# Banded window attention: softmax weights turned by a diagonal matrix of inverse row sums, V stationary, heads produced feature-major

## The reference

```python
h = shift_token(x); q, k, v = split(h @ wqkv)
q, k = l2norm(q) * qs, l2norm(k) * ksc
q, k = rotary_xpos(q, k)
sim  = einsum('bhwid,bhwjd->bhwij', 8 * q, k)   # masked to i-64 <= j <= i
attn = softmax(sim)
x    = x + reshape(attn @ v) @ wo
```

## Time and profile before

| | |
|---|---|
| median of 3 runs | 4411.17 us (4400.55 to 4414.39) |
| profiled execution | 4408.55 us |
| its span, first to last instruction | 4406.7 us |
| PE, DVE, ACT, POOL busy in the span | 78%, 74%, 54%, 57% |
| granted TensorE clock, mean | 0.897 of full speed |
| attention layer 0 of the changed function | about 1330 to 1615 us |
| attention layer 1 of the changed function | about 1670 to 1957 us |

### The profile page before, as it was taken

One profiled execution on the slowest core, in us unless ns is written; L12 is line 12 of the kernel. 1 busy time (PEld: TensorE's weight loads), 2 busy tenths in 40 slices (PEclk: granted clock), 3 DMA queues, 4 the chain that ended last, 5 costly groups with the idle time before them and its releaser, 6 DMA issues. The chain is left out here.

```text
span 4406.7 us, 82280 instructions
## 1 busy us (share of the span) xinstructions
PE 3422.4 (78%) x26525; PEld 2224.7 (50%) x26525; DVE 3282.7 (74%) x5820; ACT 2366.2 (54%) x5461; POOL 2504.6 (57%) x2258
## 2 busy tenths in 40 slices
PE   5888888888866876875879799765877776777775
PEld 3666666666654654654744577421433342333343
DVE  4777777777746865765641688678999977999995
ACT  3555555555533533442332566565777756767771
POOL 2555555555534524423420233348999965999991
PEclk8999999999977977877989899877999997999996
DMA  1000000000000000000000000017777745777760
GB/s 55 9 9 9 9 9 9 9 9 9 9 20 0 0 6 15 0 6 5 0 27 0 20 1 1 15 57 240 233 233 233 233 139 171 233 229 234 230 219 33
DMA packets 196676, 328.22 MB, mean 74 GB/s; under 512 B 96048, under 2 KB 126016, under 8 KB 194368
## 3 DMA queue, kind: packets, MB, share of 16 engines
q1 hardware_dynamic: 196288, 323.29, 23.7%
HBM read 304.30 MB, written 18.87 MB: 73 GB/s over the span
## 5 line engine op out<-in xcount | busy, mean ns | idle before, releaser
L3562 ACT ACTIVATE banks<-banks,alog 128x255 f32<-128x255 f32 x2048 | 788.6, 448 | 338.1 <-DVE h L3651 221.2
L3629 POOL TENSOR_TENSOR dBx<-residual,b_by_state 128x1024 f32<-128x1024 f32 x256 | 597.2, 2354 | 23.4 <-POOLq L3622 16.6
L3651 DVE TENSOR_TENSOR_SCAN h<-banks,dBx 128x1024 f32<-128x1024 f32 x256 | 579.8, 2281 | 35.9 <-PE banks L3491 19.7
L3629 POOL TENSOR_TENSOR norm_featmajor<-norm,b_by_state 128x1024 f32<-128x1024 f32 x256 | 597.9, 2357 | 0.5 <-DMA norm<-mamba_dtx_rows 0.5
L3651 DVE TENSOR_TENSOR_SCAN h<-banks,norm_featmajor 128x1024 f32<-128x1024 f32 x256 | 581.0, 2282 | 6.2 <-POOL norm_featmajor L3629 0.5
L3476 PE MATMUL banks<-dt_rows,selectors 128*128 128x510 bf16 x1024 | 418.0, 409 | 156.8 <-ACT banks L3562 96.3
L3491 PE MATMUL banks<-h,c_spread 128*32 128x128 f32 x8192 | 345.0, 289 | 25.0 <-DVE h L3651 18.6
L3491 PEld LDWEIGHTS banks<-h,c_spread 128*32 128x32 f32 x8192 | 203.7, 113 | 201.8 <-issue 154.4
L3474 PE MATMUL banks<-dt_rows,selectors 128*128 128x255 bf16 x512 | 151.7, 296 | 138.8 <-ACT banks L3562 134.5
L973 POOL TENSOR_TENSOR weighted<-probs,f 128x1024 f32<-128x1024 f32 x64 | 120.8, 1904 | 215.3 <-DVE f L1024 214.2
L3476 PEld LDWEIGHTS banks<-dt_rows,selectors 128*128 128x128 bf16 x1024 | 110.0, 107 | 248.2 <-ACT banks L3562 169.4
(11 more groups left out here) (455 smaller groups left out, 8994.3 us busy)
## 6 DMA issues: line engine op xcount, KB each, us to landing
residual<-mamba_dtx_rows SPq DMA_DIRECT2D x512, 256.0 KB, 3.5
norm<-mamba_dtx_rows SPq DMA_DIRECT2D x512, 256.0 KB, 3.4
mamba_dt_rows<-dt_parts SPq DMA_DIRECT2D x8, 768.0 KB, 3.4
dt_rows<-mamba_dt_rows SPq DMA_DIRECT2D x32, 192.0 KB, 4.8
delta_blocks<-A_turned SPq DMA_DIRECT2D x256, 8.0 KB, 1.5
inv_turned<-delta_blocks SPq DMA_DIRECT2D x256, 8.0 KB, 1.8
mamba_dtx_rows<-dtx SPq DMA_DIRECT2D x16, 256.0 KB, 3.7
c_spread<-in_l3a_zero SPq DMA_DIRECT2D x2, 1160.0 KB, 6.4
```

Source lines behind the costliest of these rows:

```text
L3562: e = fn(per_step(decay[l % 2])[:, 2 * x + j, 1:], k.bank[x][:, j * T + 1:(j + 1) * T], ACT.Exp, scale=mem["A"][:, at:at + 1])
L3629: nc.gpsimd.tensor_tensor(per_step(dBx[l % 4]), per_step(kept[l % 4]), across(mem["B"][:, tokens(tb)], 4), ALU.mult).then_inc(q["dbx"], 1)
L3651: v.tensor_tensor_scan(flat(h[:, u % 2, 4 * i:4 * i + 4, :]), decay[l % 2], dBx[l % 4], 0.0, ALU.mult, ALU.add).then_inc(q["scanned"], 1)
```

## The change

The turned softmax weights leave TensorE already divided by their row sums: the block of E is multiplied, as the stationary operand, by a diagonal matrix `dg` with the inverse row sums, in place of the identity. DVE inverts the sums, GpSimd multiplies the identity by them (8 diagonals of 128 x 128 for a unit, one buffer for all units). `heads_of` takes v as the stationary operand and streams ET, so the heads come out feature-major in bank 7 and go to OT by one copy; `turn_out`, `out` and the buffer O go. ACT takes over `load_x` and the third copy of ET. The orders on the engines change. The diff, cut:

```diff
 # PE
 def turn_probs(x0, b, u):
-    pe.wait_ge(q["exped"], b * NU + u + 1)
+    pe.wait_ge(q["dg_ready"], b * NU + u + 1)
...
-        i = nc.tensor.transpose(k.bank[TB + n // 4][...], E[:, u, n // 3, ...], k.ident[:])
+        i = nc.tensor.matmul(k.bank[TB + n // 4][...], E[:, u, n // 3, ...], dg[:, n // 3, (n % 3 + 1) // 2, :],
+                             start=True, stop=True)
 def heads_of(b, u):
-    pe.wait_ge(q["pt_act"], (b * NU + u) * 2 + 2)
-    pe.wait_ge(q["pt_dve"], b * NU + u + 1)
+    pe.wait_ge(q["pt_ready"], (b * NU + u) * 3 + 3)
...
-        nc.tensor.matmul(hout[:, 0, h, :], ET[:, u, 3 * h, :], v[:, 0, vh], start=True, stop=True)
-        nc.tensor.matmul(hout[:, 1, h, :], ET[:, u, 3 * h + 1, :], v[:, 0, vh], start=True, stop=False)
-        i = nc.tensor.matmul(hout[:, 1, h, :], ET[:, u, 3 * h + 2, :], v[:, 1, vh], start=False, stop=True)
+        o = k.bank[7][h % 2 * DK:(h % 2 + 1) * DK, h // 2 * T:(h // 2 + 1) * T]
+        nc.tensor.matmul(o, v[:, 0, vh], ET[:, u, 3 * h:3 * h + 2, :].rearrange("p a t -> p (a t)"),
+                         start=True, stop=False)
+        i = nc.tensor.matmul(o[:, P:T], v[:, 1, vh], ET[:, u, 3 * h + 2, :], start=False, stop=True)
-def turn_out(b, u): ...
 def step(x0, x1, x2):
-    turn_out(x2, 0)  heads_of(x2, 1)  project(x0, 0)  turn_qk(x1)  project(x0, 1)  score(x1, 0)
-    turn_out(x2, 1)  score(x1, 1)  last_projection(x2)  turn_probs(x1, 0)  heads_of(x1, 0)  turn_probs(x1, 1)
+    heads_of(x2, 1)  project(x0, 0)  turn_qk(x1)  project(x0, 1)  score(x1, 0)
+    last_projection(x2)  score(x1, 1)  turn_probs(x1, 0)  heads_of(x1, 0)  turn_probs(x1, 1)
 # ACT
+def load_x(b):
+    after(act, "proj", b * TPB)
+    for lo, at in ((0, PAD), (64, PAD - 1)):
+        nc.scalar.activation(xb[lo:lo + 64, :], ..., ACT.Copy).then_inc(q["xb_ready"], 1)
 def copy_probs(b, u):
-    for n in (0, 1):
+    for n in range(3):
 def copy_out(b, u):
-    act.wait_ge(q["o_turned"], b * NU + u + 1)
+    act.wait_ge(q["heads"], b * NU + u + 1)
 def step(x0, x1, x2):
+    load_x(x0)
     move_v(x1)
+    copy_out(x2, 1)
     read_out(x0, 0)  copy_turned(x1, 0)  copy_turned(x1, 2)  read_out(x0, 1)
-    copy_out(x2, 1)
     exponentials(x1, 0)  copy_probs(x1, 0)  exponentials(x1, 1)
+    copy_out(x1, 0)
     copy_probs(x1, 1)
-    copy_out(x1, 0)
 # POOL: front(b) is cut into squares (L1766), lengths (L1769) and turned_part (L1774)
+def weights_of(b, u):
+    pool.wait_ge(q["inverted"], b * NU + u + 1)
+    after(pool, "p_turned", (b * NU + u) * 3)
+    g.tensor_tensor(dg[:].rearrange("p h t q -> p (h t) q"), across(k.ident[:], HG * TPB),
+                    over(rs[:, u].rearrange("p h t -> p (h t)"), P), ALU.mult).then_inc(q["dg_ready"], 1)
+def step(x0, x1):
+    squares(x0)  weights_of(x1, 0)  lengths(x0)  weights_of(x1, 1)  turned_part(x0)
-front(0)
+step(0, None)
 with pool.Fori(1, B) as b:
-    front(b)
+    step(b, b - 1)
+step(None, B - 1)
 # DVE: load_x, copy_probs and out go
+def weights_of(b, u):
+    dve.wait_ge(q["exped"], b * NU + u + 1)
+    vv.reciprocal(rs[:, u], rs[:, u]).then_inc(q["inverted"], 1)
 def step(x0, x1, x2):
-    load_x(x0)  normalised(x1)  out(x2, 0)  copy_probs(x2, 1)  rotated(x1)  out(x2, 1)  copy_turned(x1)
-    norms(x0, 0)  banded(x1, 0)  maxima(x1, 0)  norms(x0, 1)  banded(x1, 1)  add_y(x2)  maxima(x1, 1)  copy_probs(x1, 0)
+    normalised(x1)  weights_of(x2, 1)  rotated(x1)  copy_turned(x1)
+    norms(x0, 0)  banded(x1, 0)  maxima(x1, 0)  norms(x0, 1)  add_y(x2)  banded(x1, 1)  maxima(x1, 1)  weights_of(x1, 0)
```

More of the change, by code:

```diff
@@ L1546, in window_attention_layer @@
                  "v_moved", "read_out", "y_added",
-                 "rotated", "turned", "t_act", "t_dve", "scores", "maxed", "exped", "p_turned", "pt_act", "pt_dve", "heads",
-                 "heads_out", "o_turned", "ot_ready", "final", "s_read")
+                 "rotated", "turned", "t_act", "t_dve", "scores", "maxed", "exped", "inverted", "dg_ready", "p_turned", "pt_ready", "heads",
+                 "ot_ready", "final", "s_read")
         q = {n: p.sem(n) for n in names}
-        hout = k.bank[7].rearrange("p (t h d) -> p t h d", t=TPB, h=HG)
         def batches(eng, step):
@@ L1588, in project @@
                     if t == 0:
-                        pe.wait_ge(q["xb_ready"], b + 1)
-                        after(pe, "pt_act", (b - 1) * NU * 2)
-                        after(pe, "pt_dve", (b - 1) * NU)
+                        pe.wait_ge(q["xb_ready"], b * 2 + 2)
+                        after(pe, "pt_ready", (b - 1) * NU * 3)
                     else:
@@ L1626, in turn_probs @@
                     else:
[L1627 to L1628 removed]
+                        after(pe, "pt_ready", (b * NU + u) * 3)
                     for n in range(HG * 3):
[L1630 to L1631 removed]
+                        i = nc.tensor.matmul(k.bank[TB + n // 4][:, n % 4 * P:(n % 4 + 1) * P],
+                                             E[:, u, n // 3, n % 3 * P:(n % 3 + 1) * P], dg[:, n // 3, (n % 3 + 1) // 2, :],
+                                             start=True, stop=True)
                         if n % 4 == 3:
@@ L1677, in step @@
                     if x2 is not None:
-                        turn_out(x2, 1)
+                        last_projection(x2)
                     if x1 is not None:
                         score(x1, 1)
-                    if x2 is not None:
-                        last_projection(x2)
                     if x1 is not None:
@@ L1691, in _ @@
             def _(act):
+                act.wait_ge(q["loaded"], 80)
+                def load_x(b):
+                    after(act, "proj", b * TPB)
+                    for lo, at in ((0, PAD), (64, PAD - 1)):
+                        nc.scalar.activation(xb[lo:lo + 64, :], k.HT[lo:lo + 64, bass.ds(b, 1), at:at + T].rearrange("p a t -> p (a t)"),
+                                             ACT.Copy).then_inc(q["xb_ready"], 1)
                 def move_v(b):
@@ L1730, in step @@
                 def step(x0, x1, x2):
+                    if x0 is not None:
+                        load_x(x0)
                     if x1 is not None:
                         move_v(x1)
+                    if x2 is not None:
+                        copy_out(x2, 1)
                     if x0 is not None:
@@ L1761, in _, with squares @@
                 pool.drain()
-                def front(b):
+                def squares(b):
                     for t in range(TPB):
@@ L1774, in front @@
                             g.tensor_tensor(qk[:, t, a], qn[:, t, a], across(tab[:, t, a, 0, :], H), ALU.mult).then_inc(q["turned_part"], 1)
-                front(0)
+                def weights_of(b, u):
[4 more added lines that the diff above has]
+                def step(x0, x1):
+                    if x0 is not None:
+                        squares(x0)
+                    if x1 is not None:
+                        weights_of(x1, 0)
+                    if x0 is not None:
+                        lengths(x0)
+                    if x1 is not None:
+                        weights_of(x1, 1)
+                    if x0 is not None:
+                        turned_part(x0)
+                step(0, None)
                 with pool.Fori(1, B) as b:
-                    front(b)
+                    step(b, b - 1)
+                step(None, B - 1)
             @block.vector
@@ L1865, in step @@
                     if x2 is not None:
-                        out(x2, 0)
-                        copy_probs(x2, 1)
+                        weights_of(x2, 1)
                     if x1 is not None:
                         rotated(x1)
-                    if x2 is not None:
-                        out(x2, 1)
-                    if x1 is not None:
                         copy_turned(x1)
```

28 lines of the change are left out of this document (6 added, 22 removed).

## The result

The changed kernel takes 4508.34 us (median of 4 runs, 4504.49 to 4509.12) against 4407.05 for the kernel before (4 runs beside it): 1.0227 times as long, 95% interval 1.0204 to 1.0249. The prediction was 4576, range 4505 to 4640, slower with 0.95; the median lies 3 above the lower end of that range, and the difference is 101 where 165 was forecast. The profiled execution took 4507.62, span 4505.8, 99.1 more than the span before (4406.7).

A forecast was written before the change was run, and what follows sets the result against it. No engine was full; a ring of waits through POOL's power set the step. Steps of 42.0 us instead of 30.98 gave 77 a layer, plus 7 for each tail, less 3: 165 more, 4576 us, range 4505 to 4640.

The forecast's parts named there:

- diagonal 0: POOL's building of unit 0's diagonal, now ahead of the power while DVE stands idle: 1.9 us a step.
- the ring: Waits in each loop step that make all four engines work one after another: 42.0 us a step instead of 30.98.
- tail of 7 a layer: Work behind a layer's last power, with two diagonals and dearer turnings, less two output detours: +7 us.
- The start: Start of layer 0, where the input copy no longer waits for POOL's memset: -2.7 us.
- power, normalising, reciprocal 1: POOL's power 5.4, DVE's normalising with its drain 3.8 and unit 1's reciprocal 0.2: 9.4 us a step.
- diagonal 1: POOL's building of unit 1's diagonal beside DVE's rotation: 2.7 us, bounds 1.9 to 3.0.
- turning 1, up to the last copy: PE's 12 turnings of unit 1's softmax weights, multiplications instead of transposes: 3.1 us at full clock, transposes 1.5.
- heads: PE's heads of unit 1, 1536 columns alternating between halves of the array: 1.9 us, formerly 2.7.
- scores to reciprocal 0: From PE's first scores through DVE's bands, maxima and sums of squares to unit 0's reciprocal: 10.0 us a step.
- more hand-overs: Some nine hand-overs between engines, most inside other terms; 0.7 us more a step.
- The clock, 4.5: PE at half clock for about ten microseconds behind its waits, partly off the critical chain: 4.5 us a step.
- Clock holds: Rival: multiplying keeps PE at 2.4 GHz on the critical chain; 37.5 us a step, 4512 total; chance 0.14.

The follow-up runs named there:

- the run with the exponentials first: Changed kernel with POOL's power before diagonal 0 and ACT's exponentials of unit 1 ahead of its copies of unit 0; 4439.21 us.
- the run with the idle multiplications: Changed kernel with multiplications nobody reads ahead of PE's waits for diagonals (18 for unit 0, 10 for unit 1); 4490.23 us, ratio 1.0195 to the kernel before.

## Why the prediction was right, and what was mis-sized

The mechanism was the one forecast, and the rows that were to show it are there: the power behind diagonal 0 of 1.89, which waits for the reciprocal; DVE idle 7.47 before normalising; PE waiting 7.33 and 4.09 ahead of the turnings. Two that were named with them are not: the power's starts are 37.5 apart and not 42, and neither turning takes 3.1 (5.13 and 4.54). The runs confirm the ring from several sides: longer diagonals lengthen the step at their full price, with none to build or wait for it is 28.8, and an earlier hand-over shortens it, except that of the power alone, behind which ACT closed the ring. That the power's place on POOL is all of it (38.1 to 39.0 with the power first), that the turning's price is (28.8 with the multiplications kept) and that TensorE's clock is (36.5 with turning 1 at full clock), each of these fell with a run. The forecast's tail of 7 a layer was right: from the last power to the MEMSET of L1343 it is 59.76 and 59.74 instead of 53.19 and 52.70, so 6.6 and 7.0 more. The start came out at -0.8 for -2.7, which the spread of that start from run to run hides.

The step was put at 42.0 and is 37.55, and 14 x 4.45 = 62 is nearly all of the 68 by which 4576 was too high. By the terms:

| term | predicted | measured |
|---|---|---|
| diagonal 0 | 1.9 | 1.85 |
| power, normalising, reciprocal 1 | 9.4 | 9.5, of it 2.5 normalising, 1.2 a wait for ACT |
| diagonal 1 | 2.7 | 2.0 |
| turning 1, up to the last copy | 3.1 | 4.6 |
| last copy | 0.6 | 0.65 |
| heads | 1.9 | 1.5 |
| projection, turn, projection | 7.2 | 7.2 |
| scores to reciprocal 0 | 10.0 | 10.2 |
| more hand-overs | 0.7 | in the rows above |
| clock | 4.5 | in turning 1 and the wait: 2.8 |

**The clock, 4.5.** This is the larger error of one term. The prediction took the earlier trace rows, where a wait is followed by transposes and then by slow heads, and carried it over: "Ten microseconds at half speed cost 5". With multiplications the slow stretch ends inside the turning. Heads and projections, which were to be slow, are not. On the ring turning 1 pays 1.6 (4.58 against the 2.98 from its start to the last copy in the run with the idle multiplications, where it has full clock). A second share came by a way that the prediction ruled out: it called the turning of unit 0 "off the ring", but that turning's delay passes through ACT's copies and exponentials to reciprocal 1, which waits 1.22. "Clock holds", with its 4512, was nearest in its number and had 0.14; its ground, that transposes and multiplications differ for the clock, was the right one, and the earlier trace rows showed transposes alone. But the clock did not hold in either turning: that its step of 37.5 meets the measured 37.55 is luck, a sum 2.75 too high without the 2.8 that the clock cost.

**The rest, 2.75.** At full clock the sum of 37.5 should have been 34.75: normalising takes 2.5 and not 3.8 (its four products 2.50 with GpSimd idle beside them, 3.58 in the earlier trace rows, 4.18 beside a diagonal in the run with the power first); diagonal 1 takes 2.0 and not 2.7; heads 1.5 and not 1.9; the rest is mostly hand-overs counted twice. For diagonal 1 the prediction looked for the price on the wrong engine: GpSimd's instruction kept its length, and DVE's rotation, now beside it and beside all of the turned part behind it, went from 4.32 to 8.73. That it ends just in time was foreseen ("the one covers the other with little to spare"): it ends at 1518.76, PE turns q and k at 1519.02. The run with the idle multiplications showed that this cover is the next bound.

## What to carry to other kernels

Where an engine that works in order already holds one link of a ring, a new job that waits for a late input holds that link back as well. Give the job to another engine, or a place with nothing of the ring behind it: here the same change costs 101 us with the diagonals on GpSimd and gains 26 with them on DVE and three jobs moved. Order alone, with the diagonals still on GpSimd, gave back 69. Ask of each new wait who stands behind it on that engine, and follow the delay through every engine until it comes back to its start, ACT's queue included. A slow-clock stretch that is read behind transposes says little of the same place filled with multiplications.

## What the runs showed of the hardware

- Behind a wait of 4.05, 12 FP32 transposes left TensorE at 1.2 GHz (2.82, and the heads behind them 2.81), where multiplications of the same blocks brought it back to 2.4 within the turning behind one of 4.09 (4.54, the heads 1.50); the granted clock of a step was 0.68 and 0.82. At full clock the transposes take 1.52 and the multiplications 2.94.
- GpSimd's tensor operations lengthen DVE's. DVE's eight products of L1827 took 2.72 in the run with the exponentials first, where GpSimd waited for most of them, 4.32 in the kernel before (L1814 there) with GpSimd busy for 2.0 of that time, and 8.73 in the kernel after with GpSimd busy for 7.5 of it; GpSimd's diagonal took 1.89 with DVE idle and 1.90 beside that. It is not always GpSimd that goes first: its four of L1776 took 5.68 in the kernel after and 6.88 with DVE building the diagonals. The Trainium skill's page "SBUF — State Buffer", "SBUF: two separate sides", says that VectorE and GpSimd share one pair of ports under an exclusive lock, the later one waiting for a whole instruction. The growth from 2.72 to 8.73, 6.0 of the 7.5 for which GpSimd was busy, agrees with a lock.
- Heads that alternate between two halves of the array's columns took 1.50 for 1536 columns (1514.84 to 1516.34), where a tile's projection, also 1536 columns, took 2.68. That two heads overlap fits this, but no run takes the halves apart.
